# Adjacency residual network on one core: new orders at the first queries, two block seams and the last tiles

## The reference, cut to what matters

```python
# block 0: two graph attention layers
proj = x @ W; Wh, Ws = split(proj, 2)
a = softmax(Wh @ Ws.T) * adj
x = leaky_relu(a @ Wh + x)
# block 1: relu(((A_norm @ x) @ W)),   A_norm = D^-1/2 (adj + I) D^-1/2
# block 2: relu((adj / deg) @ x @ W_neigh.T + x @ W_self.T + biases)
# block 3: h = relu(adj @ (x @ W1) + b1);  out = adj @ (h @ W2) + b2     (W1: 256 x 128, W2: 128 x 256)
```

## Time and profile before

| what | us |
|---|---|
| median of three runs | 736.05 |
| the three runs | 735.72, 736.05, 737.24 |
| the profiled execution | 736.77 |
| its span in the trace | 735.0 |
| its mean granted PE clock | 0.997 of full speed |

### The profile page before, as it was taken

One profiled execution on the slowest core, in us unless ns is written; L12 is line 12 of the kernel. 1 busy time (PEld: TensorE's weight loads), 2 busy tenths in 40 slices (PEclk: granted clock), 3 DMA queues, 4 the chain that ended last, 5 costly groups with the idle time before them and its releaser, 6 DMA issues.

```text
span 735.0 us, 13241 instructions
## 1 busy us (share of the span) xinstructions
PE 719.0 (98%) x3984; PEld 613.1 (83%) x3984; DVE 481.4 (66%) x1111; ACT 337.3 (46%) x785; POOL 324.6 (44%) x346
## 2 busy tenths in 40 slices
PE   8999999999999999999999999999999999989995
PEld 7888888888888888888888888888777687779985
DVE  3767777777776664655755755754677848875366
ACT  4666565665656455365465465451222412221121
POOL 1157676676766316454454454384664000003200
PEclk9999999999999999999999999999999999999998
DMA  7042424324242201732231232246862222210012
GB/s 271 29 144 93 166 87 144 113 101 156 86 153 76 111 18 58 166 119 74 87 128 71 86 128 72 86 103 126 194 171 87 72 64 66 66 44 2 1 44 74
DMA packets 63139, 72.39 MB, mean 98 GB/s; under 512 B 36336, under 2 KB 56432, under 8 KB 58992
## 3 DMA queue, kind: packets, MB, share of 16 engines
q1 hardware_dynamic: 63088, 71.78, 31.3%
HBM read 46.60 MB, written 16.78 MB: 86 GB/s over the span
## 4 chain that ended last, share of the span: by engine, by line
PE 93%; DVE 3%; issue 1%; ACT 1%; POOL 1%; DMA 0%; SPq 0%; DVEq 0%; POOLq 0%; ACTq 0%
PE scores L1901 39%; PE ob L1901 29%; PE tb L1901 11%; PE tb L2070 7%; PE xb L1901 3%; PE tb L2014 1%; DMA self_term_scratch<-rst 0%; PE tb L1920 0%; PE xb L2095 0%; PE xb L1949 0%; POOL adjr L648 0%; SPq L477 0%; DVE xt_l L1222 0%; PE scores L2371 0%; DVE zb L1611 0%
## 5 line engine op out<-in xcount | busy, mean ns | idle before, releaser
L671 POOL TENSOR_TENSOR prob<-prob,arow 128x512 f32<-128x512 f32 x128 | 191.9, 1521 | 145.9 <-ACT prob L875 145.8
L1901 PE MATMUL ob<-val,stationary 128*128 128x512 f32 x960 | 186.7, 344 | 0.0
L1901 PEld LDWEIGHTS ob<-val,stationary 128*128 128x128 f32 x960 | 146.7, 189 | 18.4
L1222 DVE TENSOR_TENSOR stationary<-tb,stationary 128x512 fp32r<-128x512 f32 x128 | 85.4, 687 | 57.3 <-ACT stationary L776 56.1
L1901 PE MATMUL scores<-wst_h,whs_h 128*128 128x512 f32 x256 | 102.6, 401 | 0.0
L1901 PE MATMUL scores<-wst_h,whs_l 128*128 128x512 f32 x256 | 100.0, 390 | 0.0
L1901 PE MATMUL scores<-wst_l,whs_h 128*128 128x512 f32 x256 | 99.8, 390 | 0.0
L1319 DVE TENSOR_REDUCE row_values<-scores 128x1 f32<-128x512 f32 x128 | 85.9, 683 | 13.5 <-PE scores L1901 12.0
L776 ACT ACTIVATE stationary<-tb 128x512 fp32r<-128x512 f32 x128 | 72.9, 595 | 42.4 <-PE tb L2070 40.9
L875 ACT ACTIVATE prob<-scores,row_values 128x512 f32<-128x512 f32 x128 | 86.8, 690 | 11.4 <-DVE row_values L1326 11.4
L2070 PE MATMUL tb<-ident,prob 128*128 128x128 f32 x512 | 71.7, 272 | 0.0
(11 more groups left out here) (227 smaller groups left out, 1191.7 us busy)
## 6 DMA issues: line engine op xcount, KB each, us to landing
arow<-in_adj SPq DMA_DIRECT2D x32, 1024.0 KB, 5.2
adjacency_halves<-arow SPq DMA_DIRECT2D x16, 512.0 KB, 3.0
features_scratch<-xs SPq DMA_DIRECT2D x32, 128.0 KB, 1.9
xres<-features_scratch SPq DMA_DIRECT2D x32, 128.0 KB, 2.1
keep<-in_x SPq DMA_DIRECT2D x4, 512.0 KB, 7.2
xres<-in_x SPq DMA_DIRECT2D x16, 128.0 KB, 2.0
self_term_scratch<-rst SPq DMA_DIRECT2D x16, 128.0 KB, 1.7
rin<-self_term_scratch SPq DMA_DIRECT2D x16, 128.0 KB, 2.2
```

Of the source, the lines that this page charges most:

```text
L671: nc.gpsimd.tensor_tensor(prob[u][:, cs], prob[u][:, cs], arow[u][:, cs], ALU.mult).then_inc(g.msk.sem, 1)
L1222: return nc.vector.tensor_tensor(dst, v, h.bitcast(F32), ALU.subtract)
L1901: return nc.tensor.matmul(o, l, r, start=start, stop=stop)
```

## The change

It re-orders instructions and re-groups one sum; the numbers computed stay the same.

* `keep_busy(3)` goes, and the wait for `wg_l` at the head of layer 0 too. `first_queries` makes both query banks at once, in the order in which operands appear: high by high of k = 0, then of k = 1, `wg_h` by `xtall_l` of k = 0, the four products with `wg_l`, and last `wg_h` by `xtall_l` of k = 1.
* In `body` the steps are spread over 47 chunks in place of 48. The pairs then stand after chunks (2,4), (6,7), (9,11), (12,14), (16,17), (19,21), (22,24), (26,27), (29,31), (32,34), (36,37), (39,41), (42,44) and (46,47).
* Seam from block 1 to 2: on PE two chunks of block 2 stand ahead of `C_rows` of tile 14; on DVE `split(0)` stands ahead of `residual` of tile 14, and `split(1)` behind `total` of tile 15 and `rows_lo` of tile 14.
* Seam from block 2 to 3: four chunks of E stand ahead of `D_rows` of tile 14 and three more (one of them for tile 2 alone) ahead of `D_project` of tile 14; the last products of tiles 2 and 3 are placed ahead of the last of tiles 0 and 1.
* F has groups of 4, 4, 3, 3 and 2 row tiles, a new table of places for `F_project`, a new `LEAD`, and on DVE a new order: `sums_lo` of the last two groups stands behind `statistics`, and the operations of tiles 13, 14 and 15 are written out.

```diff
@@ -214,10 +214,10 @@
         BANKS = len(sums)
 
 
-        GROUPS = [(0, 4), (4, 8), (8, 12), (12, 14), (14, 16)]
+        GROUPS = [(0, 4), (4, 8), (8, 11), (11, 14), (14, 16)]
         fbank = sums + [xb[0]]
         pbank = jb + [xb[1]]
-        LEAD = [0, 4, 8, 11, 13]
+        LEAD = [0, 4, 8, 10, 13]
         finished = xs + xres
 
         passed = {e: sem(f"waits_passed_{e}") for e in ("sync", "gpsimd", "scalar", "vector")}
@@ -1834,20 +1834,31 @@
                             moving_lo(*pp)
 
                     if a is F:
-                        for t in range(NT + 1):
+                        for t in range(NT - 2):
                             y, z = (t // 2 * 2, t % 2), ((t - 1) // 2 * 2, (t - 1) % 2)
-                            if t in LEAD:
+                            if t in LEAD and t <= TPC * 2:
                                 sums_lo(LEAD.index(t))
-                            if t < NT:
-                                with_residual(*y)
+                            with_residual(*y)
                             if t:
                                 inverse(*z)
-                            if t < NT:
-                                statistics(*y)
+                            statistics(*y)
+                            if t in LEAD and t > TPC * 2:
+                                sums_lo(LEAD.index(t))
                             if t:
                                 normed(*z)
-                            if t < NT:
-                                mean_variance(*y)
+                            mean_variance(*y)
+                        inverse(NT - 4, 1)
+                        normed(NT - 4, 1)
+                        with_residual(NT - 2, 0)
+                        statistics(NT - 2, 0)
+                        with_residual(NT - 2, 1)
+                        mean_variance(NT - 2, 0)
+                        statistics(NT - 2, 1)
+                        inverse(NT - 2, 0)
+                        mean_variance(NT - 2, 1)
+                        normed(NT - 2, 0)
+                        inverse(NT - 2, 1)
+                        normed(NT - 2, 1)
                         continue
                     if a is E:
                         for t in range(NT):
@@ -1864,16 +1875,16 @@
                     if not a.last:
                         total(NT - 2, 0)
                         rows_lo(NT - 4, 1)
-                        residual(NT - 2, 0)
                         if a is C:
                             split(0)
+                        residual(NT - 2, 0)
                         norm(NT - 2, 0)
                         self_term(NT - 4, 1)
                         moving_lo(NT - 4, 1)
+                        total(NT - 2, 1)
+                        rows_lo(NT - 2, 0)
                         if a is C:
                             split(1)
-                        total(NT - 2, 1)
-                        rows_lo(NT - 2, 0)
                         residual(NT - 2, 1)
                         norm(NT - 2, 1)
                         if a is C:
@@ -1940,7 +1951,6 @@
 
             keep_busy(8)
             features(0)
-            keep_busy(3)
 
             def n_rows(t, u):
                 pe.wait_ge(n_new, t + 1)
@@ -1963,8 +1973,8 @@
                 pe.sem_inc(g.wsl.sem, 1)
                 pe.sem_inc(g.staged.sem, 1)
                 pe.sem_inc(g.vl.sem, 1)
-                pe.wait_ge(s_wgl[l], 1)
                 if l:
+                    pe.wait_ge(s_wgl[l], 1)
                     ge(pe, G[l - 1].ex, 4 * NT)
 
                 def rows_turned(i):
@@ -1977,23 +1987,38 @@
                 def project_part(i, o, bank):
 
                     gs, os = bass.ts(i, CH), slice(o * P, (o + 1) * P)
-                    if not l and isinstance(i, int) and i + o == 0:
-
-                        for k in range(KT):
-                            pe.wait_ge(s_x0l, k + 1)
-                            mm(bank[:, :], wg_h[:, k, os], xtall_h[:, k, gs], k == 0, False)
-                            mm(bank[:, :], wg_h[:, k, os], xtall_l[:, k, gs], False, False)
-                            last = mm(bank[:, :], wg_l[:, k, os], xtall_h[:, k, gs], False, k == KT - 1)
-                        last.then_inc(g.prod.sem, 1)
-                        return
                     exact3(bank[:, :], [(wg_h[:, k, os], wg_l[:, k, os], xtall_h[:, k, gs], xtall_l[:, k, gs])
                                         for k in range(KT)]).then_inc(g.prod.sem, 1)
 
+                def first_queries():
+
+                    def both(w, x, k, start=False):
+                        return [mm(scores[:, o * CH:(o + 1) * CH], w[:, k, o * P:(o + 1) * P], x[:, k, 0:CH],
+                                   start, False) for o in range(KT)]
+
+                    pe.wait_ge(s_wqh, 1)
+                    for k in range(KT):
+                        pe.wait_ge(s_x0h, k + 1)
+                        both(wg_h, xtall_h, k, k == 0)
+                    pe.wait_ge(s_x0l, 1)
+                    both(wg_h, xtall_l, 0)
+                    pe.wait_ge(s_wgl[0], 1)
+                    for k in range(KT):
+                        both(wg_l, xtall_h, k)
+                    pe.wait_ge(s_x0l, KT)
+                    for o in range(KT):
+                        mm(scores[:, o * CH:(o + 1) * CH], wg_h[:, 1, o * P:(o + 1) * P], xtall_l[:, 1, 0:CH],
+                           False, True).then_inc(g.prod.sem, 1)
+
                 def project(i):
 
                     if l or i:
                         rows_turned(i)
+                    else:
+                        first_queries()
                     for o in range(2 * KT):
+                        if not l and isinstance(i, int) and i == 0 and o < KT:
+                            continue
                         if not l and o == KT:
                             features(i + 1)
                             if i == 0:
@@ -2428,12 +2453,12 @@
                             step, i = next(ended)
                             step(*tile(i))
 
-                    parts, total = NCH * (NT - BANKS), 2 * (NT - 2)
+                    parts, total = NCH * (NT - BANKS) - 1, 2 * (NT - 2)
                     for t in range(BANKS, NT):
                         for c in range(NCH):
                             chunk(k, c, t)
-                            if project:
-                                n = NCH * (t - BANKS) + c
+                            n = NCH * (t - BANKS) + c
+                            if project and n < parts:
                                 steps((n + 1) * total // parts - n * total // parts)
 
                 chunk(0, 0, 0, 1, 2, 3)
@@ -2445,10 +2470,10 @@
                 end_sums(0, NT - NCH)
                 body(0, C_rows, C_project)
 
+                chunk(1, 0, 0, 1)
                 C_rows(NT - 2, 0)
-                chunk(1, 0, 0, 1)
+                chunk(1, 0, 2, 3)
                 C_project(NT - 2, 0)
-                chunk(1, 0, 2, 3)
                 chunk(1, 1, 0, 1)
                 C_rows(NT - 2, 1)
                 chunk(1, 1, 2, 3)
@@ -2457,25 +2482,30 @@
                 end_sums(1, NT - NCH)
                 body(1, D_rows, D_project)
 
+                chunk(2, 0, 0, 1)
+                chunk(2, 1, 0, 1)
                 D_rows(NT - 2, 0)
-                chunk(2, 0, 0, 1)
+                chunk(2, 2, 0, 1)
+                chunk(2, 0, 2)
                 D_project(NT - 2, 0)
-                chunk(2, 0, 2, 3)
-                chunk(2, 1, 0, 1, 2, 3)
-                chunk(2, 2, 0, 1)
+                chunk(2, 0, 3)
+                chunk(2, 1, 2, 3)
                 D_rows(NT - 2, 1)
                 chunk(2, 2, 2, 3)
-                for t in range(BANKS):
+                for t in range(2):
                     sum_over(2, t, NT - 4, NT - 2)
                 D_project(NT - 2, 1)
-                for t in range(BANKS):
-                    sum_over(2, t, NT - 2, NT - 1)
-                end_sums(2, NT - 1)
+                for t in range(2, BANKS):
+                    sum_over(2, t, NT - 4, NT - 1)
+                for t in range(2):
+                    sum_over(2, t, NT - 2, NT)
+                for t in range(2, BANKS):
+                    sum_over(2, t, NT - 1, NT)
                 body(2, None, None)
 
                 across_sums(0, 0, NT)
-                for q, steps in ((1, {3: 0, 6: 1, 9: 2, 12: 3}), (2, {3: 4, 6: 5, 9: 6, 12: 7}),
-                                 (3, {5: 8, 9: 9, 13: 10}), (4, {2: 11, 8: 12, 13: 13})):
+                for q, steps in ((1, {3: 0, 6: 1, 9: 2, 12: 3}), (2, {3: 4, 6: 5, 10: 6, 13: 7}),
+                                 (3, {4: 8, 8: 9, 12: 10}), (4, {5: 11, 9: 12, 13: 13})):
                     for j in range(NT):
                         across_sums(q, j, j + 1)
                         if j in steps:
```

## The result

The changed kernel takes 731.24 us (median of 4 runs, 730.93 to 731.55) against 736.64 for the kernel before (735.72 to 737.67): a ratio of 0.9926, interval 0.9909 to 0.9943. Forecast 730.4, range 729.4 to 733.2. Measured again on another chip it was 731.59 (731.34 to 731.78) against 736.43, ratio 0.9936 (0.9922 to 0.9949). The profiled execution took 731.1 with a span of 729.3; 731.1 and 729.35 were forecast for it. The sum fits better than its terms, as the rest shows.

What follows compares the result with a forecast made beforehand. PE, busy for 98% of the span, was taken as the bound, so only its waits and the tail could be won. Gains of 1.0 + 1.75 + 2.4 + 0.5 = 5.65 us gave 730.4 us, range 729.4 to 733.2.

Steps and rivals of the forecast that it cites:

- First queries: Start of the kernel: second group of transposes at 10.03 instead of 11.08 us, gain taken as 1.0, low end 0.
- rival of the lost start: Start: removed keep_busy products had raised PE's rate, so the start loses 1.3; gain 3.35, 732.7 us; chance 0.10.
- Bodies: Bodies of blocks 1 and 2, steps spread over 47 chunks: losses of 0.1 and 0.25 us taken.
- The wait of 0.3: Block 2's body: a step moves by 0.92 us with 0.6 to spare, so PE must wait some 0.3.
- DVE's pace: Block 2's end: DVE finishes tile 15 at 3.99 us a tile regardless; seam gives 1.2, total gain 4.45, 731.6; chance 0.14.
- Seam from block 1 to 2: Between blocks 1 and 2: PE's waits for tile 14's rows and their remainder close; gain 1.85 us, with the body 1.75.
- my working on `split(0)` and the square root: Block 1 to 2: split(0) first bares the square root's 0.44 us; tile 14 normalised by 581.26, before PE needs it at 581.41.
- Seam from block 2 to 3: Between blocks 2 and 3: most of 3.6 us of PE's waits close; gain 2.4 us, ends 1.2 and 2.8.
- Last tiles: Block 3's end, new groups and DVE order: gain 0.5 us, ends -0.3 and 0.9.
- PE's work in F stays about the same: F's products: 64 of 384 columns cost 11.0 to 11.5 us against 11.2 replaced; difference taken as 0.
- the tail: End, from the last sums' remainder on DVE to the last tile's normalisation: 4.38 us instead of 4.84.
- The sum: Whole kernel: 1.0 + 1.75 + 2.4 + 0.5 = 5.65 us gained, forecast 730.4 us, chance 0.55.

## Why the prediction was right, step by step

**First queries: right.** 1.0 was taken. Like has to be set beside like here, by the point at which the full clock's record begins. Where that is at about 7 us or later, the second transposes come at 11.06 and 11.08 with the old start and at 10.12 to 10.16 with the new one: a gain of 0.90 to 0.96. Where it is at about 6, they come at 11.05 and at 9.80: 1.25. Where it is at 5.05 or earlier, at 10.57 and at 9.56 or 9.20: 1.0 to 1.4, and there the products wait for the weights instead (0.67 above). So about 0.5 of the 1.52 between the first two traces is chance, the clock's and not the change's. The Trainium skill (TensorE: Matmul & The Clock Gate, Part 1: The HAM clock gate) says that the point at which the clock rises varies from run to run of one kernel. The traces agree: in the changed kernel's two it is 4.76 and 7.76 us, in all fourteen 4.50 to 7.76. That the time ahead of it is spent at the lower level is read from the durations, which are twice as long, for no record covers it.

The rival of the lost start is answered by the same record. In two traces without the removed products the clock was up at 4.50 and 4.76, ahead of the first transposes, and in all nine it was up by 7.76; so the removed products were not needed for the rise, which the prediction had left open. In three of the nine it came at 7.52 to 7.76, later than in any trace with them (7.07 at the latest). But the second transposes were then at most 0.04 later than with a rise at 7.08 (10.16 against 10.12), not 2.3.

**Bodies: block 1 right, block 2 too small.** Taken -0.1 and -0.25. Block 1: 103.47 with 48 slots (one trace), 103.56 to 103.70 with 47 in six traces without further waits, so -0.1 to -0.2. Block 2: 63.69 to 63.90 with 48, 64.18 to 64.30 with 47: -0.5. Two steps failed there. The wait of 0.3 that was expected ahead of tile 13's transposes is not there: its row is normalised at 648.21 + 0.41 = 648.62 and turned at 649.23, with the same 0.6 to spare as before, because DVE's row and PE's step both came earlier. And the list of places that pay was too short. I counted the pairs with a single chunk between `rows` and `project`, five for four, some 0.26 for the one more. Between a projection and the next tile's `rows` a single chunk stands four times in either spacing; before, two of the four lost some 0.23 to a row that DVE had not yet normalised, and after, all four do (644.78 above; tile 12 before lost 0.06). Two more such waits and the one pair more, 2 x 0.17 + 0.26 = 0.6, account for the 0.5. So DVE's pace did bind, not at tile 15 as that rival said but between steps of the body.

**Seam from block 1 to 2: right in size, wrong in one reason.** 1.85 without the body; 105.28 - 103.47 = 1.81 for two traces without waits in the body. The same is won with VectorE's old order, so my working on `split(0)` and the square root decided nothing.

**Seam from block 2 to 3: right, but for the clock.** 2.65 without the body; 2.68 in the trace of that seam alone. The two distances that the forecast took over from the earlier trace rows, from tile 15's projection to its operand and from there to the first free bank, came out as they were: 660.80 - 659.13 = 1.67 and 661.90 - 660.80 = 1.10. With the body 2.13 in the trace after, 2.4 forecast: the body cost 0.25 more than was taken. Not forecast at all: the seam's waits let the clock fall in a fifth of the runs, 18/89 x 1.43 = 0.3 us in the mean, which the new seam wins besides and which a trace without a fall can't show. With the 2.68 that comes to the 3.0 measured for the seam alone, whose interval (2.3 to 4.2 us) is too wide to prove this sum.

**Last tiles: wrong, by its sign.** +0.5 was taken, -0.3 at the least; it costs 0.5 by the run without it, 1.0 by the run of it alone. Two steps failed. "PE's work in F stays about the same" was right by the price (0.176 for a 384-column product), but eight shorter products cover 1.41 us of ACT's copy and DVE's subtraction where they covered 1.82, so the projection of tile 4, which used to go through in 0.36, takes 0.58, waiting for its remainder; and that of tile 8, which the table places after the fifth operand instead of the sixth, takes 0.67 instead of 0.55. 64 x 0.176 = 11.3 against 32 x (0.23 + 0.12) = 11.2 leaves the larger part of the 0.4 to these waits. And the tail was followed to the last normalisation alone. That is 0.53 earlier (3.37 or 3.38 us behind PE's last product start, 3.91 or 3.92 with the old order), but from there to the end of the span are 3.9 to 4.3 us in six traces with the new order and 3.0 to 3.8 in eight with the old, 4.1 and 3.5 in the mean: nothing is left. The time goes into the last store: from its issue to its landing are 2.9 to 3.3 us with the new order, 2.0 to 2.9 with the old. The last two tiles are ready 0.63 apart instead of 1.04; that their stores hinder each other is argued, not shown.

**The sum.** By like-with-like terms, with the smaller gain of the start, it is 0.95 + 1.7 + 2.15 - 0.5 + 0.3 = 4.6, against 4.6 to 5.4 measured beside three sets of runs of the kernel before (the lowest with VectorE's old order at the first seam). The forecast of 5.65 was a little high because of the last tiles, and its own execution, 5.7, came out by chance: 0.5 from an early rise of the clock, and a wait of 0.28 in block 1's body that of the two first traces only the one before had.

## What to carry to other kernels

Follow a change to the end of the span, not to the last arithmetic: two tiles finished earlier but closer together lost their gain in the last store here. When steps are packed closer, check each kind of neighbour, before and behind each step, against the time at which the engine that feeds it is ready. And run each part alone and the whole without it: here three good changes, the start and the two seams, hid two bad ones, the last tiles and block 2's spacing, and the version without these two was faster.

## What was not expected of the hardware

The granted clock fell to 0.50 after TensorE had stood still 1.46 and 0.38 us with two transposes and eight 256-column products between, in one trace and not in the three others with the same two waits; it cost 1.43 us. At the start, the full clock's record began at 4.76 us in one execution of the changed kernel and at 7.76 in another. The time from the last normalisation to the end of the span varied from 3.0 to 3.8 us between executions with the same order there, and it is the last store's landing that varied. All three are as large as the terms that a prediction of this kind adds up.
